# The last attention head and the feed-forward part of a transformer block: another order of steps, a longer lag, and the last two tiles ended one by one

## The chip, the cores and the metric

The kernel runs on one core of one Trainium2 chip. The metric is the time of the program on the device in microseconds, of which the median of three runs stands below. TensorE (PE) multiplies matrices into eight banks of PSUM, VectorE (DVE), ScalarE (ACT) and GpSimd (POOL) do the rest, and SyncE (SP) issues the DMAs. Each engine works off a list of its own in order, and waits on semaphores for the others.

## The reference

One transformer block with its norms behind it, on 1024 tokens of 256 features: 16 attention heads over compressed keys and values, a small sparse attention whose mean is added to the heads, an output projection, a layer norm, a feed-forward part with ternary weights, and a second layer norm. What the change touches is the last of it:

```python
scores = jnp.where(causal[None, None], -jnp.inf, scores)
probs = jax.nn.softmax(scores, axis=-1)
attn = jnp.einsum('bhqk,bhkd->bhqd', probs, v)
...
out = attn.transpose(0, 2, 1, 3).reshape(B, S, NH * VD) @ W_o
...
x = _layernorm(x + attention)
up = jnp.einsum('bsd,ed->bse', x, wu)
gate = jnp.einsum('bsd,ed->bse', x, wg)
hidden = jax.nn.silu(up) * gate
x = _layernorm(x + jnp.einsum('bse,de->bsd', hidden, wd))
```

Here wu, wg and wd are the weights rounded to -1, 0 and 1, times their mean absolute value.

## The kernel before

Everything is float32. Where a product must be exact enough, an operand is held as a high part (rounded to the fast matmul format fp32r) and a low part, and two or three matmuls are added up; so many tiles exist as a pair `Xh`, `Xl`. ScalarE writes the high part out of PSUM by a copy, and VectorE the low part by a subtraction (line 1058 or 1235).

**Order of the work.** The program is a list of steps, written out by hand, that every engine walks through: each step is a tuple (kind, head offset, c), and each engine has, for each kind, its share of instructions and waits. So a step that moves in the list moves on all engines at once. The heads come in pairs; a prologue, the first pair, a loop over six pairs and the last pair `LAST` use `head_steps`, and `EPILOGUE` holds what is left of head 15 and the feed-forward part. A head has eight slots, one for each tile of 128 queries. Slot i is

```python
s += [("qk", h, i), *slots[i][:e], ("exp", h, i), *slots[i][e:]]
```

with e = 2, so two steps stand between a score tile and its exponential.

**Steps of a head.** `qk` i: five matmuls for each 512 keys into SC0 or SC1, and VectorE's masked maximum (line 1121). `exp` i: ScalarE's exponential into Pb (line 959). `tc`: transposes of up to four blocks of Pb on TensorE (line 701), `PTh` by ScalarE, `PTl` by VectorE; tiles 4 to 7 have two such steps each. `pv` g: the product with V for query tiles 2g and 2g+1 (lines 675 to 677), `ATh` and `ATl`. `wo` g: the product with the output weights, and VectorE adds it to `acc` (lines 1270 and 1276). A banked step uses the next of four PSUM banks J0 to J3 and waits until that bank's step four places before has been read.

**Layer norm and feed-forward part.** `ln1` c: statistics of tokens 256c to 256c+255 on VectorE (1218, 1222), then an addition and a power on GpSimd (605, 607). `ln1n` c: VectorE normalises `acc` (1227). `ht` c, for c = 0 and 1, and `h2` c, for 2 and 3: four transposes of the normalised tokens (831, 891), ScalarE's two copies and VectorE's two subtractions (1235), which give `hTh` and `hTl`; these live in the buffers QNh0, QNl0 and QS0, KD0. The steps n = 0 to 31 are 8 blocks of 128 hidden features for each of four groups of 256 tokens:

- `ug` n: eight matmuls, up and gate, into a half of SC0 or SC1 (866, 867). It waits for hidden step n-4; `ug` 0 and 1 also wait for the exponential of tile 6, `ug` 2 and 3 for that of tile 7.
- `m` n, the hidden step: ScalarE's sigmoid (988), then the copy `Hh` of step n-1 (941; names RKh, RKl); VectorE's two products (1191 `QX`, 1194 `CS`); GpSimd's subtraction `Hl` (640; names RQh, RQl). Hh and Hl are rings of eight.
- `dn` n, the down product: four matmuls into J0 and J1 or J2 and J3 (883, 884), added up over eight n. In the list it stands LAG = 5 steps behind `ug`.
- `res`, `ost`, `onorm` q, for two tiles of tokens each: VectorE adds `acc` (1198), takes statistics (1203, 1206), GpSimd makes the inverse deviation, VectorE normalises (1212), and SyncE stores 256 KB (541).

The sigmoid needs another table than the exponential; its load (ACT_TABLE_LOAD) is put directly before the first sigmoid.

## Time and profile before

| | us |
|---|---|
| median of three runs | 727.49 (726.06 to 728.73) |
| the profiled run | 727.64 |
| span of the profiled run | 725.9 |
| TensorE busy | 665.2 (92%) |
| VectorE busy | 469.2 (65%) |
| ScalarE busy | 397.7 (55%) |
| GpSimd busy | 365.8 (50%) |

Times within the execution are counted from the start of the span. A row of the order of time gives start, length, engine, line, operation and tiles, and in square brackets how long the engine stood idle before it and what ended that. Matmuls overlap: a row of 0.28 us is followed by the next 0.12 later. The profile names tiles by their buffers, so the hidden tiles read as RKh, RQh and so on, and the tokens' transposes as QNh, QNl, QS and KD.

### The profile page before, as it was taken

How to read it: one execution, taken by the hardware profiler on the slowest of the kernel's cores; microseconds unless marked ns; L12 is line 12 of the kernel's file. 1: busy time of each engine (PE TensorE's matmuls, PEld its weight loads, DVE VectorE, ACT ScalarE, POOL GpSimd, SP SyncE). 2: the span in 40 equal slices, each digit the busy share in tenths (PEclk: the TensorE clock that was granted, in tenths of full speed). 3: DMA queues.
4: the chain of work that ended last, by engine and by line, in shares of the span. 5: the costliest groups of instructions: out<-in, count | busy, mean ns of one | idle time of the engine just before them, and what ended most of it. 6: DMA issues, size and time to landing. Idle time of an engine off the chain costs nothing.

```text
span 725.9 us, 14196 instructions
## 1 busy us (share of the span) xinstructions
PE 665.2 (92%) x4496; PEld 604.1 (83%) x4496; DVE 469.2 (65%) x1293; ACT 397.7 (55%) x940; POOL 365.8 (50%) x313
## 2 busy tenths in 40 slices
PE   5666799999999999999999999999999999898895
PEld 5646689888988898889888888898889888887895
DVE  2675256666766576666666666666656677895895
ACT  3342254756475647565656565656565658544562
POOL 5522254835474447445744575356536644530563
PEclk9866599999999999999999999999999999999998
DMA  6142310371036103710361037103610373000000
GB/s 203 46 130 75 79 51 1 88 154 52 1 89 153 51 0 87 152 51 0 87 152 51 0 87 152 51 0 87 151 51 0 87 217 87 2 1 1 1 31 30
DMA packets 28719, 50.51 MB, mean 70 GB/s; under 512 B 8976, under 2 KB 19472, under 8 KB 28688
## 3 DMA queue, kind: packets, MB, share of 16 engines
q1 hardware_dynamic: 28688, 50.12, 27.5%
q8 instruction: 17, 0.28, 0.2%
q14 instruction: 14, 0.11, 0.1%
HBM read 15.50 MB, written 1.05 MB: 23 GB/s over the span
## 4 chain that ended last, share of the span: by engine, by line
PE 60%; DVE 13%; ACT 12%; issue 10%; POOL 4%; DMA 1%; DVEq 0%; ACTq 0%; POOLq 0%; SPq 0%
PE J L675 10%; PE J L677 9%; PE J L676 9%; PE J L701 4%; DVE PTl L1058 4%; ACT kvraw L1022 3%; PE SC L692 3%; PE SC L690 3%; PE SC L689 3%; PE SC L691 3%; PE SC L688 3%; POOL rstd L607 3%; ACT Pb L959 3%; ACT PTh L941 2%; PE SC L866 2%
## 5 line engine op out<-in xcount | busy, mean ns | idle before, releaser
L1058 DVE TENSOR_TENSOR PTl<-J,PTh 128x512 fp32r<-128x512 f32 (+1 forms) x192 | 102.5, 554 | 75.1 <-ACT PTh L941 74.4
L959 ACT ACTIVATE Pb<-SC,nm 128x128 f32<-128x128 f32 (+7 forms) x128 | 94.8, 740 | 47.0 <-DVE nm L1121 46.2
L1121 DVE CUSTOM_DVE_ANT_0 SC<-SC,mask 128x128 f32<-128x128 f32 (+7 forms) x128 | 97.4, 761 | 28.7 <-PE SC L692 27.1
L941 ACT ACTIVATE PTh<-J 128x512 fp32r<-128x512 f32 (+1 forms) x192 | 88.3, 492 | 10.3 <-PE J L701 9.5
L701 PE MATMUL J<-ident,Pb 128*128 128x128 f32 x576 | 88.0, 280 | 4.7 <-ACT Pb L959 4.5
L675 PE MATMUL J<-PTh,Vh 128*128 128x256 f32 x320 | 88.0, 275 | 4.0 <-DVE PTl L1058 3.8
L676 PE MATMUL J<-PTl,Vh 128*128 128x256 f32 x320 | 89.6, 280 | 0.0
L677 PE MATMUL J<-PTh,Vl 128*128 128x256 f32 x320 | 89.3, 279 | 0.0
L701 PEld LDWEIGHTS J<-ident,Pb 128*128 128x128 f32 x576 | 64.8, 142 | 11.2 <-ACT Pb L959 5.4
L688 PE MATMUL SC<-KNh,QNh 128*128 128x512 f32 (+1 forms) x192 | 69.1, 360 | 0.0
L675 PEld LDWEIGHTS J<-PTh,Vh 128*128 128x128 f32 x320 | 60.2, 188 | 9.0 <-DVE PTl L1058 6.7
L690 PE MATMUL SC<-KNh,QNl 128*128 128x512 f32 (+1 forms) x192 | 66.8, 348 | 0.0
L689 PE MATMUL SC<-KNl,QNh 128*128 128x512 f32 (+1 forms) x192 | 66.8, 348 | 0.0
L692 PE MATMUL SC<-KL,QS 128*128 128x512 f32 (+1 forms) x192 | 66.8, 348 | 0.0
L691 PE MATMUL SC<-KD,QS 128*128 128x512 f32 (+1 forms) x192 | 66.7, 347 | 0.0
L941 ACT ACTIVATE ATh<-J 128x256 fp32r<-128x256 f32 x64 | 24.5, 383 | 73.1 <-PE J L677 72.4
L676 PEld LDWEIGHTS J<-PTl,Vh 128*128 128x128 f32 x320 | 60.3, 188 | 0.6
L677 PEld LDWEIGHTS J<-PTh,Vl 128*128 128x128 f32 x320 | 60.6, 190 | 0.0
L1058 DVE TENSOR_TENSOR ATl<-J,ATh 128x256 fp32r<-128x256 f32 x64 | 27.0, 422 | 49.5 <-ACT ATh L941 49.5
L1276 DVE SCALAR_TENSOR_TENSOR acc<-J,rs,acc 128x256 f32<-128x256 f32 x128 | 56.1, 480 | 2.6
L941 ACT ACTIVATE kvraw<-J 128x512 f32<-128x512 f32 x32 | 19.2, 599 | 65.6 <-PE J L677 65.6
L1022 ACT ACTIVATE kvraw<-kvraw,nmr,rstd 128x128 f32<-128x128 f32 x128 | 52.6, 487 | 2.5 <-POOL nmr L654 2.5
(267 smaller groups left out, 1916.7 us busy)
## 6 DMA issues: line engine op xcount, KB each, us to landing
KD<-RKh SPq DMA_DIRECT2D x32, 256.0 KB, 4.5
KL<-RKl SPq DMA_DIRECT2D x32, 256.0 KB, 5.1
KX<-KX SPq DMA_DIRECT2D x16, 256.0 KB, 2.4
QX<-QX SPq DMA_DIRECT2D x16, 256.0 KB, 2.4
QS<-RQh SPq DMA_DIRECT2D x16, 256.0 KB, 4.0
QS<-RQl SPq DMA_DIRECT2D x16, 256.0 KB, 4.5
r_kv<-in_L_attn_W_ckv SPq DMA_DIRECT2D x8, 384.0 KB, 3.4
r_qn<-in_L_attn_W_qT SPq DMA_DIRECT2D x16, 128.0 KB, 2.7
```

The source lines that it names most:

```text
L675: mm(o, lhsT=wh, rhs=xh, start=start, stop=False)
L676: mm(o, lhsT=wh, rhs=xl, start=False, stop=False)
L677: return mm(o, lhsT=wl, rhs=xh, start=False, stop=stop)
L688: mm(o[:, k], lhsT=QNh[b][:, q], rhs=KNh[b][:, k], start=True, stop=False)
L689: mm(o[:, k], lhsT=QNh[b][:, q], rhs=KNl[b][:, k], start=False, stop=False)
L690: mm(o[:, k], lhsT=QNl[b][:, q], rhs=KNh[b][:, k], start=False, stop=False)
L692: last = mm(o[:, k], lhsT=QS[b][:, q], rhs=KL[b][:, k], start=False, stop=True)
L701: last = pe.transpose(o[:, tile(j - 4 * c)], Pb[i % 2][:, tile(j)], ident[:, :])
L941: return act.activation(o, i, ACT.Copy)
L959: act.activation(Pb[i % 2][:, w], SC[i % 2][:, w], ACT.Exp, bias=nm[:, i % 2:i % 2 + 1], scale=-1.0, accum_out=sm[:, b, i:i + 1]).then_inc ...
L1058: dve.tensor_tensor(o, i, h.bitcast(F32), ALU.subtract).then_inc(done[kind], 1)
L1121: dve.tensor_tensor_reduce(out=SC[i % 2][:, w], in0=SC[i % 2][:, w], in1=mask[:, 128 * (7 - i):S], scale=-SCALE, scalar=HIGH, op0=ALU.add, ...
```

## The change

1. In the last head, `ln1 0` moves from slot 5 to 4, `ln1n 0` from 6 to 5, `ht 0` from 7 to 6, and `ug 0` and `ug 1` from the epilogue into slot 7, ahead of `ln1n 1`.
2. The epilogue begins with `wo 2`, the transposes of tile 7, `ug 2`, `ht 1`, `m 0` and `ug 3`, and `pv 3` comes behind `m 0`; the sigmoid's table load moves with `m 0`.
3. LAG is 7 instead of 5. `dn 0` comes behind `ug 7`, and eight down products stand behind `ug 31` where six stood.
4. `m 31` comes ahead of `res 2`, `ost 2` and `onorm 2`, and the last two tiles of tokens have steps of their own: `last 0` and `last 1` (sum, statistics; on GpSimd the inverse deviation of one tile) and `lnorm 0` and `lnorm 1` (normalise one tile, store 128 KB). TensorE signals tile 6 with a semaphore of its own, `dn_first`, in the middle of `dn 31`.

The core of the diff:

```diff
-LAG = 5
+LAG = 7
...
-                    add(5, True, ("ln1", 0, 0))
-                    add(6, True, ("ln1n", 0, 0), ("ln1", 0, 1))
-                    add(7, True, ("ht", 0, 0), ("ln1n", 0, 1))
+
+            def late_steps():
+
+                add(4, True, ("ln1", 0, 0))
+                add(5, True, ("ln1n", 0, 0))
+                add(6, True, ("ht", 0, 0), ("ln1", 0, 1))
+                add(7, True, ("ug", 0, 0), ("ug", 0, 1), ("ln1n", 0, 1))
...
             if last:
                 mlp_steps()
+                if b == 1:
+                    late_steps()
...
-            if q >= 1:
+            if q in (1, 2):
                 a += {1: [one("res", q - 1)], 2: [one("ost", q - 1)], 4: [one("onorm", q - 1)]}.get(e, [])
...
-        EPILOGUE = [one("ug", 0), one("ug", 1), *t(NH - 1, 7), ("wo", NH - 1, 2), one("ht", 1), ("pv", NH - 1, 3), one("m", 0),
-                    one("ln1", 2), one("ug", 2), one("ug", 3), one("m", 1), ("wo", NH - 1, 3), one("ln1n", 2), one("ug", 4),
-                    one("m", 2), one("ln1", 3), one("ug", 5), one("m", 3), one("dn", 0), one("ug", 6), one("ln1n", 3),
-                    one("m", 4), one("dn", 1)]
+        EPILOGUE = [("wo", NH - 1, 2), *t(NH - 1, 7), one("ug", 2), one("ht", 1), one("m", 0), one("ug", 3), ("pv", NH - 1, 3),
+                    one("m", 1), one("ln1", 2), one("ug", 4), one("m", 2), ("wo", NH - 1, 3), one("ln1n", 2), one("ug", 5),
+                    one("m", 3), one("ln1", 3), one("ug", 6), one("m", 4), one("ln1n", 3)]
         for n in range(7, NM):
             EPILOGUE += mlp_steps_of(n)
-        EPILOGUE += [one("m", NM - 2), one("onorm", 2), one("m", NM - 1)] + [one("dn", n) for n in range(NM - LAG, NM)]
-        EPILOGUE += [one("res", 3), one("ost", 3), one("onorm", 3)]
+        EPILOGUE += [one("m", NM - 2), one("dn", NM - 7), one("m", NM - 1), one("res", 2), one("ost", 2), one("onorm", 2)]
+        EPILOGUE += [one("dn", n) for n in range(NM - 6, NM)] + [one("last", 0), one("last", 1), one("lnorm", 0), one("lnorm", 1)]
...
+                    if kind == "last":
+                        q = slice(6 + c, 7 + c)
+                        inv_std(mv2[:, q, 1], ve2[:, q], rsd2[:, q], y_ag, c + 4, y_ve, y_rsd, c + 4)
...
+                    if n == NM - 1 and t == 0:
+                        last.then_inc(dn_first, 1)
...
+                    if kind == "last":
+                        t = 6 + c
+                        dve.wait_ge((dn_first, dn_ready)[c], (1, NM)[c])
+                        dve.scalar_tensor_tensor(yo[:, t, :], J[2 + c][:, 0:D], scl[:, 2:3], acc[:, t, :],
+                                                 ALU.mult, ALU.add).then_inc(y_done, 1)
+                        dve.wait_ge(y_done, t + 1)
+                        dve.bn_stats(st2[:, t, :], yo[:, t, :]).then_inc(y_st, 1)
+                        dve.wait_ge(y_st, t + 1)
+                        dve.bn_aggr(mv2[:, t, :], st2[:, t, :]).then_inc(y_ag, 1)
```

TensorE, from the transposes of tile 6 to the last product with V, first before and then after. `ident,acc` are the transposes `ht` (the first of them in the row before; after the change it stands some thirty rows further up, not shown), `SC0<-` and `SC1<-` the up products, `ident,Pb0` and `ident,Pb1` the transposes of tiles 6 and 7, `ABh1,ATh0` the output product 2, and `PTh,Vh1` the products with V. Line numbers of after are 12 to 14 higher.

```order
L701 MATMUL J3<-ident,Pb0 128x128 x4
L701 MATMUL J0<-ident,Pb0 128x128 x3
L831 MATMUL J1<-ident,acc 128x128 x4
L866 MATMUL SC0<-QNh0,xTh 128x256
...
L867 MATMUL SC0<-KD0,xTl 128x256
L701 MATMUL J2<-ident,Pb1 128x128 x4
L701 MATMUL J3<-ident,Pb1 128x128 x4
L675 MATMUL J0<-ABh1,ATh0 128x256
...
L831 MATMUL J1<-ident,acc 128x128 x4
L675 MATMUL J2<-PTh,Vh1 128x256
```

```order
L713 MATMUL J0<-ident,Pb0 128x128 x4
L713 MATMUL J1<-ident,Pb0 128x128 x3
L878 MATMUL SC0<-QNh0,xTh 128x256
...
L879 MATMUL SC0<-KD0,xTl 128x256
L687 MATMUL J2<-ABh1,ATh0 128x256
...
L713 MATMUL J3<-ident,Pb1 128x128 x4
L713 MATMUL J0<-ident,Pb1 128x128 x4
L878 MATMUL SC1<-QNh0,xTh 128x256
...
L843 MATMUL J1<-ident,acc 128x128 x4
L878 MATMUL SC1<-QNh0,xTh 128x256
...
L687 MATMUL J2<-PTh,Vh1 128x256
```

Before, `ht 0` stands between the transposes of tile 6 and up product 0; after, up products 0 and 1 follow these transposes directly, output product 2 stands ahead of the transposes of tile 7, and up products 2 and 3 stand ahead of the last product with V.

ScalarE, from the copy of tile 7's transposes to the first sigmoids, before and after. `QNh0` and `QNl0` are the copies of `ht 1`, `ATh1` that of the last product with V, `QX<-SC0,scl` the sigmoids.

```order
L941 ACTIVATE PTh<-J2 128x4x128
L941 ACTIVATE PTh<-J3 128x4x128
L941 ACTIVATE QNh0<-J1 128x256
L941 ACTIVATE QNl0<-J1 128x256
L941 ACTIVATE ATh1<-J2 128x256
L988 ACT_TABLE_LOAD
L988 ACTIVATE QX<-SC0,scl 128x256 x2
```

```order
L955 ACTIVATE PTh<-J1 128x3x128
L955 ACTIVATE PTh<-J3 128x4x128
L955 ACTIVATE PTh<-J0 128x4x128
L955 ACTIVATE QNh0<-J1 128x256
L955 ACTIVATE QNl0<-J1 128x256
L1002 ACT_TABLE_LOAD
L1002 ACTIVATE QX<-SC0,scl 128x256
L955 ACTIVATE ATh1<-J2 128x256
L1002 ACTIVATE QX<-SC0,scl 128x256
```

The table load and sigmoid 0 stood behind `ATh1` and now stand ahead of it.

VectorE, the end of its list, before and after. `QX` and `CS` are a hidden step, `KX<-J` the sum with `acc`, `KX<-KX` the normalisation.

```order
L1206 BN_AGGR mv<-st 128x2 x2
L1191 SCALAR_TENSOR_TENSOR QX<-SC,scl,QX 128x256
L1194 SCALAR_TENSOR_TENSOR CS<-SC,scl,QX 128x256
L1212 TENSOR_SCALAR KX<-KX,mv,rsd 128x256 x2
L1191 SCALAR_TENSOR_TENSOR QX<-SC,scl,QX 128x256
L1194 SCALAR_TENSOR_TENSOR CS<-SC,scl,QX 128x256
L1198 SCALAR_TENSOR_TENSOR KX<-J,scl,acc 128x256 x2
L1203 BN_STATS st<-KX 128x6 x2
L1206 BN_AGGR mv<-st 128x2 x2
L1212 TENSOR_SCALAR KX<-KX,mv,rsd 128x256 x2
```

```order
L1208 SCALAR_TENSOR_TENSOR CS<-SC,scl,QX 128x256
L1212 SCALAR_TENSOR_TENSOR KX<-J,scl,acc 128x256 x2
L1217 BN_STATS st<-KX 128x6 x2
L1220 BN_AGGR mv<-st 128x2 x2
L1240 TENSOR_SCALAR KX<-KX,mv,rsd 128x256 x2
L1225 SCALAR_TENSOR_TENSOR KX<-J,scl,acc 128x256
L1228 BN_STATS st<-KX 128x6
L1230 BN_AGGR mv<-st 128x2
L1225 SCALAR_TENSOR_TENSOR KX<-J,scl,acc 128x256
L1228 BN_STATS st<-KX 128x6
L1230 BN_AGGR mv<-st 128x2
L1234 TENSOR_SCALAR KX<-KX,mv,rsd 128x256 x2
```

Before, hidden step 31 stands behind the normalisation of tiles 4 and 5; after, sum, statistics and normalisation of tiles 4 and 5 stand behind it, and tiles 6 and 7 follow one by one.

## Rows read from the trace of the kernel before

**Rows 1.** The page, parts 1 and 2: span and granted clock in 40 slices.

```profile
span 725.9 us, 14196 instructions
...
PEclk9866599999999999999999999999999999999998
```

**Rows 2.** Windows: us, busy (x instructions) of TensorE, its weight loads, VectorE, ScalarE, GpSimd; clock; DMA.

```profile
48.00:52.00 4.00, 3.84 (x11) 3.09 (x12) 3.87 (x7) 0.61 (x2) 0.00 (x0) 0.64 0.00 0
...
655.90:658.70 2.80, 0.09 (x1) 0.00 (x0) 2.02 (x6) 1.99 (x5) 0.00 (x0) 1.00 0.00 0
...
660.00:663.40 3.40, 3.40 (x19) 3.40 (x17) 0.41 (x1) 0.79 (x2) 0.00 (x0) 0.51 0.00 0
```

**Rows 3.** Order of time, TensorE, 650 to 668: start, length, engine, line, operation [idle <-releaser].

```profile
650.24 0.40 PE L688 MATMUL SC<-KNh,QNh 128*128 128x512 f32 x1
...
654.61 0.95 PE L701 MATMUL J<-ident,Pb 128*128 128x128 f32 x7
...
655.39 0.60 PE L831 MATMUL J<-ident,acc 128*128 128x128 f32 x4
...
658.73 0.39 PE L866 MATMUL SC<-QNh,xTh 128*128 128x256 f32 x1 [2.74 <-DVE KD L1235]
...
664.68 0.36 PE L675 MATMUL J<-PTh,Vh 128*128 128x256 f32 x1 [0.15 <-DVE PTl L1058]
...
667.53 0.33 PE L866 MATMUL SC<-QNh,xTh 128*128 128x256 f32 x1
```

**Rows 4.** Order of time, TensorE, in the prologue, the last pair and the feed-forward part.

```profile
48.16 0.47 PE L675 MATMUL J<-qch,Wqph 128*128 128x512 f32 x1 [1.98 <-DVE qcs L1058]
...
631.63 0.36 PE L675 MATMUL J<-PTh,Vh 128*128 128x256 f32 x1 [1.12 <-DVE PTl L1058]
...
679.77 0.39 PE L866 MATMUL SC<-QNh,xTh 128*128 128x256 f32 x1 [0.33 <-DVE CS L1194]
...
684.62 0.28 PE L866 MATMUL SC<-QNh,xTh 128*128 128x256 f32 x1
...
713.03 0.27 PE L866 MATMUL SC<-QNh,xTh 128*128 128x256 f32 x1
...
713.97 0.28 PE L883 MATMUL J<-KNh,RKh 128*128 128x256 f32 x1
...
718.83 0.38 PE L883 MATMUL J<-KNl,RKl 128*128 128x256 f32 x1 [1.90 <-POOL RQl L640]
```

**Rows 5.** Order of time, VectorE, 648 to 683.

```profile
648.61 0.29 DVE L1058 TENSOR_TENSOR PTl<-J,PTh 128x128 fp32r<-128x128 f32 x1 [0.35 <-ACT PTh L941]
...
668.15 0.42 DVE L1058 TENSOR_TENSOR ATl<-J,ATh 128x256 fp32r<-128x256 f32 x1 [1.89 <-ACT ATh L941]
...
670.86 0.74 DVE L1218 BATCH_NORM_STATS2 st<-acc 128x6 f32<-128x256 f32 x2
...
672.95 0.88 DVE L1276 SCALAR_TENSOR_TENSOR acc<-J,rs,acc 128x256 f32<-128x256 f32 x2
...
677.65 1.16 DVE L1227 TENSOR_SCALAR acc<-acc,mvl,rsd 128x256 f32<-128x256 f32 x2 [0.40 <-POOL rsd L607]
...
681.42 0.47 DVE L1191 SCALAR_TENSOR_TENSOR QX<-SC,scl,QX 128x256 f32<-128x256 f32 x1
...
682.33 0.47 DVE L1191 SCALAR_TENSOR_TENSOR QX<-SC,scl,QX 128x256 f32<-128x256 f32 x1
```

**Rows 6.** Order of time, ScalarE, last exponential and table load.

```profile
655.76 1.11 ACT L959 ACTIVATE Pb<-SC,nm 128x1024 f32<-128x1024 f32 x1
...
668.13 1.28 ACT L988 ACT_TABLE_LOAD   x1
```

**Rows 7.** Order of time, ScalarE and VectorE, from the last sigmoid to the end.

```profile
714.17 0.48 ACT L988 ACTIVATE QX<-SC,scl 128x256 f32<-128x256 f32 x1 [0.60 <-PE SC L867]
...
719.60 0.88 DVE L1198 SCALAR_TENSOR_TENSOR KX<-J,scl,acc 128x256 f32<-128x256 f32 x2 [2.08 <-PE J L884]
...
722.54 0.74 DVE L1212 TENSOR_SCALAR KX<-KX,mv,rsd 128x256 f32<-128x256 f32 x2 [1.19 <-POOL rsd L607]
```

More of the change, by code:

```diff
@@ L240, in attention_and_mlp @@
                                                                   sem("hid_done"), sem("hh_done"), sem("hl_done"))
+        dn_first = sem("dn_first")
         dn_ready, y_done, y_st, y_ag, y_ve, y_rsd, y_ln, stored = (sem("dn_ready"), sem("y_done"), sem("y_st"),
@@ L538, in run @@
                         sp.dma_start(raw[c].rearrange("p (k n) -> p k n", n=src.shape[2]), src).then_inc(ld_mlp[c], 16)
+                    if kind == "lnorm":
+                        sp.wait_ge(y_ln, c + 4)
+                        sp.dma_start(out[768 + 128 * c:896 + 128 * c, :], yo[:, 6 + c, :]).then_inc(stored, 16)
                     if kind == "onorm":
@@ L548, in _ @@
             run(EPILOGUE, 0)
-            sp.wait_ge(stored, 64)
+            sp.wait_ge(stored, 80)
         LD_C, LD_SIDE, LD_W0 = 16 * 8, 16 * 8, 16 * 7
@@ L1207, in run @@
                         ins.then_inc(y_ag, 1)
+                    if kind == "last":
[7 more added lines that the diff above has]
+                        dve.bn_aggr(mv2[:, t, :], st2[:, t, :]).then_inc(y_ag, 1)
+                    if kind == "lnorm":
+                        t = 6 + c
+                        dve.wait_ge(y_rsd, c + 4)
+                        dve.tensor_scalar(yo[:, t, :], yo[:, t, :], mv2[:, t, 0:1], rsd2[:, t:t + 1], ALU.subtract,
+                                          ALU.mult).then_inc(y_ln, 1)
                     if kind == "onorm":
```

## The prediction

> **What bounds the kernel now.** I read the page first: the span is 725.9 us, and the clock row reads 9 of 10 in every slice behind the prologue but the last [rows 1]; a drop of some 3 us inside a slice of 18 does not show there, so finer windows are needed. The change touches nothing before the last head, at about 640 us, so I then read the engines' order of time from there to the end. The reader is to see four stretches in it.
>
> First, TensorE runs dense through the last score tile, the third product with V and the transposes, and then stands still for 2.74 us before up product 0, released by VectorE's `KD`, the low half of the transposed tokens [rows 3]. `KD` is late because the step `ht 0` stands behind the last exponential, which starts at 655.76 [rows 6]. Second, that stall drops the clock: 0.51 of full speed from 660.0 to 663.4, at 3.40 of 3.40 us busy, after 0.09 of 2.80 us busy [rows 2]. That is the level of 1.2 GHz instead of 2.4, and it loses half of 3.4 us, 1.7 us. Third, from 668 to 680 the feed-forward part starts up: up product n waits for hidden step n-4, VectorE makes one hidden step per 0.91 us [rows 5], with the layer norms, the last output product and the splits between them, and TensorE waits for it. The last such wait is of 0.33 us, at 679.77 [rows 4]. Fourth, from there to 713.03 TensorE is dense: 20 steps (one up, one down product each) from 684.62 to 713.03 are 1.42 us each [rows 4]. At the end down product 31 waits 1.90 us for the chain of hidden step 31 [rows 4], and the output norm of two tiles and a store follow.
>
> **The transposed tokens and two up products come forward.** Nothing is added here; the steps change places on all engines. From the start of the last score tile at 650.24 [rows 3] I lay the new order with the old durations: `ht 0` 0.48 (its row at 655.39 is busy 0.60 with 0.12 of overlap), score tile, product with V and seven transposes 5.15 (655.39 less 650.24), up products 0 and 1 at 0.94 each (713.97 less 713.03, [rows 4]), output product 2 at 0.79 (six matmuls at 0.119, the rate of the 24 from 664.68 to 667.53, and 0.08 to begin), eight transposes 0.9 (seven took 0.78 from 654.61), up product 2, `ht 1` 0.48, up product 3, and the last product with V 2.85. It ends at 664.65, where before it ended at 667.53.
>
> Is each input there? `ht 0` on TensorE waits for the first layer norm, which VectorE and GpSimd now make one slot earlier; VectorE's idle pieces in that slot, such as 0.35 us at 648.61 [rows 5], take the 0.95 us that come in, and the norm ends about 649.9, 0.3 before it is asked for. Its copies stand on ScalarE between the exponential of tile 6 and that of tile 7, its splits on VectorE ahead of the last score's reduction: 0.67 us more there, but the norm of tiles 0 and 1 has left that place (0.69), so the last exponential slips by the 0.4 us that TensorE's own order adds, from 655.76 to about 656.2, done at 657.4. The eight transposes ask for it at 658.5. `KD` is there at about 653.6, up product 0 asks at 655.9: the 2.74 us stall goes, and with it the clock drop behind it. The cover is therefore 1.1 us at the exponential and 2.3 us at `KD`; where one is gone, the excess is paid one to one.
>
> **The sigmoid's table.** Its load takes 1.28 us and stood straight behind the copy of the last product with V [rows 6], so VectorE waited for the first sigmoid. Now it stands behind `ht 1`, whose copies end about 661.6; sigmoid 0 can start at 662.9 and hidden step 0 ends at 664.4, while TensorE is busy to 664.65 with the last product with V. The load costs nothing there, with 0.25 us to spare. The Trainium skill, "ScalarE: Activation LUTs", section "What ACT_TABLE_LOAD costs", counts about 2.66 us for a switch, with a drain. The row here has 1.28; by the page's price the sum would be about 1.1 us worse.
>
> **The start-up is then VectorE's.** Before, the split `ATl` of the last product with V began at 668.15 [rows 5], 0.62 behind the last matmuls of that product, and hidden step 7 ended at 683.32 (682.33 and 0.51 and 0.48). Now `ATl` begins at 665.27 and VectorE is free at 665.65. What it has to do up to hidden step 7: seven hidden steps (1 to 7) at 0.91, two layer-norm statistics at 0.94 (two of 0.74 busy and aggregates), one output add with its reciprocal 1.05, one normalisation 0.69 without and one 1.08 with GpSimd beside it, and with 0.40 of waiting for GpSimd's `rsd` (677.65), one split pair 0.67 [rows 5]: 12.1 us. Hidden step 7 ends at 677.8, 5.5 us earlier. Lag 7 takes down products 0 and 1 out of this stretch, which TensorE spends waiting anyway. Up product 9 starts behind hidden step 5, at 675.35; with down 2, the `h2` transposes, up 10 and down 3 (0.94, 0.48, 0.48, 0.94, 0.48) up product 11 starts at 678.65. It started at 684.62: **5.97 us earlier**, 0.95 of it work that the lag has put off to the end.
>
> In this stretch TensorE idles for about 0.75 and then 1.55 us around up products 6 and 7. An idle of 2.74 us dropped the clock; so did one of 1.98 (0.64 over 48 to 52 [rows 2, 4]); one of 1.12 did not [rows 4]. Ours lie between, close together, so I take a drop as somewhat likelier than not. It would fall where TensorE has slack, and laying up 7, down 0 and `h2` at half speed I find 0.4 us of loss, up to 1.0 if it comes two products later. I take **0.4** and keep 0 to 1.7.
>
> **The middle.** The 20 steps stay at 1.42 us: VectorE needs 8 x 0.91 and about 2.6 for the output norm per eight steps, 9.9 against TensorE's 11.4. The ring of eight hidden tiles allows lag 7: when ScalarE writes tile n, down product n-8 has been issued before up product n. Up product 31 starts at 713.03 - 5.97 + 0.4 = 707.46.
>
> **The end.** With eight down products behind up product 31 (3.8 us), the chain of hidden step 31 is there before TensorE asks for it, so its 1.90 us wait goes. But what is late next? VectorE: `last 0` stands behind `onorm 2`, which waits for GpSimd behind `res 2` and `ost 2`. From sigmoid 31, 1.14 behind the start of up product 31 (714.17 [rows 7]), now at 708.6: sigmoid and hidden step 1.42; `res 2` with its statistics 1.76 and GpSimd 1.18 (719.60 to 722.54, of which the last 1.18 are the wait for `rsd` [rows 7]); `onorm 2` 0.66; `last 0` and `last 1`, one after the other in three dependent operations each (0.48, 0.41, 0.17 and gaps of 0.04), 1.1 each; GpSimd 1.18; `lnorm 1` 0.43; store 2.62 (725.9 less 723.28). That is 11.45 us where 11.73 stood (725.9 less 714.17): **0.3 us** gained. TensorE is done 2.5 us before `last 1` starts, so ending the tiles one by one earns nothing by itself; the end gains since up product 31 no longer has 0.95 us of down products before it, which is in the 5.97. The halved last store is not in the trace; I take it at the full one's price, since that is the nearest row, with -0.5 to +0.3 as bounds. The extra store and GpSimd's two more pairs lie under `last 1`.
>
> **Sum.** 5.97 - 0.4 + 0.3 = 5.9 us. The profiled run took 727.64, 1.7 more than its span and 0.15 above the median of 727.49; from the median the forecast is **721.6 us**.
>
> **The rivals.**
> - The forecast, 720.3 to 722.8: chance 0.60. For it speaks that each stall has a releaser whose new place is known.
> - Better, 719.4 to 720.3: the clock holds and the smaller store lands sooner. Chance 0.12.
> - The first sigmoid is late: `ht 1` slips past the 0.25 us of cover, and hidden step 0 falls into VectorE's full stretch, at 0.91 and up to the 1.3 us of a load before it: 723.8 at most. Chance 0.05.
> - The switch holds ScalarE longer than the load's own row, say for twice its 1.28 us: 1.1 us past the cover, 722.7. Against it: between the copy before the load and the load there is no gap. Chance 0.05. (By the table page of the Trainium skill named above, this is what a switch costs.)
> - The clock costs more, or VectorE's stretch does: a second drop before up product 11, or one reaching into the dense part, 1.7 us each, or VectorE slowed by GpSimd: 723.3 to 725. Chance 0.08.
> - The change doesn't do what it says: the order of waits in ScalarE's queue (the `ht 0` copies stand ahead of the copy of the product with V and of the last exponential) gives back what the earlier start earns. It costs 4 us only if the norm's end slips from 649.9 to 654; then 725.5 to 729. Chance 0.06.
> - Slower: the clock drops around 671 and stays down. At 48 to 52 it was low with 3.84 of 4 us busy [rows 2], so being busy again does not at once lift it. Each us at half costs 0.5 once TensorE is the bound; it eats the 5.9 and 2.2 more when it lasts 16 us, giving 730 and above. Against it: the drop of 660.0 ended after 3.4 us of the same kind of matmuls. Chance 0.04.
>
> **The numbers.** About 0.3% (2.2 us) is what a measurement of this kernel tells from no change. Faster by more than that: the first five, 0.90; within it 0.06; slower 0.04. The range 719.5 to 724.6 leaves out the last two, the top of the fifth and a tip of the second.
>
> **What would show it.** After: no idle above 0.5 us between the last score tile and the last product with V, and full clock there; table load near 661.6; hidden step 7 ending near 677.8 and up product 11 starting near 679; no wait of TensorE behind up product 31; VectorE, not TensorE, ahead of `last 0`, and about 11.4 us from sigmoid 31 to the end. Wrong would be: a stall before `ht 0` near 650, a low clock in the dense part, or a hidden step 0 behind the last product with V.

## The result, and the profile after

The changed kernel takes **719.58 us**, the median of nine runs (717.91 to 724.32), where the kernel before, run nine times beside it, takes 727.49 (724.88 to 728.73). The ratio is 0.991, with a 95% interval of 0.989 to 0.993: 6.4 us less, 4.9 to 7.8. The profiled execution took 718.92 us. From its page, the lines that answer to [rows 1]:

```profile
span 717.1 us, 14199 instructions
...
PEclk9866599999999999999999999999999999999998
```

The spans differ by 8.8 us (725.9 less 717.1), more than the ratio says. To see why, I split both executions at a mark: VectorE's reduction of the score tile of queries 768 to 895 in the last head. Of what the change moves, only the statistics and the normalisation of the first layer norm (`ln1 0`, `ln1n 0`) stand ahead of it, and the times below show that they cost nothing there. A row ahead of it is the first score tile of all. The order of time, before and then after:

```profile
84.77 0.31 PE L688 MATMUL SC<-KNh,QNh 128*128 128x128 f32 x1
...
649.77 1.10 DVE L1121 CUSTOM_DVE_ANT_0 SC<-SC,mask 128x896 f32<-128x896 f32 x1
```

```profile
82.22 0.31 PE L700 MATMUL SC<-KNh,QNh 128*128 128x128 f32 x1
...
647.20 1.09 DVE L1135 CUSTOM_DVE_ANT_0 SC<-SC,mask 128x896 f32<-128x896 f32 x1
```

So 2.57 us of the 8.8 were there at the mark, and 2.55 already at the first score tile, where the two kernels issue the same things; the last section says what they are. **Behind the mark it is 76.13 us before (725.9 less 649.77) and 69.90 after**, 6.2 less. All that follows is counted from this mark, so that what an execution wins or loses in the prologue stays out.

TensorE, the rows that answer to [rows 3, 4]: up product 0, the two waits of the start-up (ahead of up products 6 and 7), up products 11 and 31, and the down products' last part:

```profile
653.27 0.36 PE L878 MATMUL SC<-QNh,xTh 128*128 128x256 f32 x1
...
665.83 0.38 PE L878 MATMUL SC<-QNh,xTh 128*128 128x256 f32 x1 [0.62 <-DVE CS L1208]
...
668.48 0.54 PE L878 MATMUL SC<-QNh,xTh 128*128 128x256 f32 x1 [1.44 <-DVE CS L1208]
...
676.70 0.28 PE L878 MATMUL SC<-QNh,xTh 128*128 128x256 f32 x1
...
705.12 0.27 PE L878 MATMUL SC<-QNh,xTh 128*128 128x256 f32 x1
...
709.78 0.28 PE L896 MATMUL J<-KNl,RQl 128*128 128x256 f32 x1
```

The 2.74 us before up product 0 are gone, and so are the 1.90 us before down product 31; the two waits that are left between the last score tile and the end are of 0.62 and 1.44 us. The windows, to set beside [rows 2]:

```profile
655.90:658.90 3.00, 3.00 (x28) 3.00 (x28) 2.78 (x7) 1.54 (x4) 0.00 (x0) 1.00 0.00 0
...
668.80:671.80 3.00, 3.00 (x15) 3.00 (x15) 2.54 (x8) 0.85 (x3) 2.44 (x4) 0.50 0.00 0
...
675.00:705.00 30.00, 30.00 (x257) 30.00 (x255) 26.18 (x63) 18.44 (x48) 18.80 (x27) 1.00 0.06 19
```

Where the clock had fallen before, it is full. It falls now behind the wait of 1.44 us: 0.50 over three busy us, 15 matmul rows where the window above has 28. From 675 to 705 TensorE is busy without a gap, at full clock.

ScalarE, the table load, the first sigmoid and the last ([rows 6, 7]), and then VectorE: the low half of the tokens' transposes, the split `ATl`, the last normalisation of a layer norm, hidden step 7, and the end ([rows 5, 7]):

```profile
659.12 1.28 ACT L1002 ACT_TABLE_LOAD   x1
660.41 0.47 ACT L1002 ACTIVATE QX<-SC,scl 128x256 f32<-128x256 f32 x1
...
706.26 0.47 ACT L1002 ACTIVATE QX<-SC,scl 128x256 f32<-128x256 f32 x1 [0.64 <-PE SC L879]
```

```profile
650.52 0.42 DVE L1263 TENSOR_TENSOR KD<-J,QNl 128x256 fp32r<-128x256 f32 x1
...
662.57 0.42 DVE L1072 TENSOR_TENSOR ATl<-J,ATh 128x256 fp32r<-128x256 f32 x1 [0.65 <-ACT ATh L955]
...
670.64 1.16 DVE L1255 TENSOR_SCALAR acc<-acc,mvl,rsd 128x256 f32<-128x256 f32 x2 [0.39 <-POOL rsd L616]
...
674.98 0.48 DVE L1208 SCALAR_TENSOR_TENSOR CS<-SC,scl,QX 128x256 f32<-128x256 f32 x1
...
710.61 0.73 DVE L1240 TENSOR_SCALAR KX<-KX,mv,rsd 128x256 f32<-128x256 f32 x2 [1.18 <-POOL rsd L616]
711.26 0.48 DVE L1225 SCALAR_TENSOR_TENSOR KX<-J,scl,acc 128x256 f32<-128x256 f32 x1
...
712.33 0.45 DVE L1225 SCALAR_TENSOR_TENSOR KX<-J,scl,acc 128x256 f32<-128x256 f32 x1
...
714.57 0.41 DVE L1234 TENSOR_SCALAR KX<-KX,mv,rsd 128x256 f32<-128x256 f32 x1 [0.71 <-POOL rsd L616]
```

The last four rows are the end: VectorE waits 1.18 us for GpSimd inside `onorm 2` and goes on to `last 0` and `last 1`, whose down products TensorE had done at 710.06 (709.78 and 0.28). The last store follows the row of 714.57.

### The profile page after: what moved, and what is told of

Its sections match the earlier page's. It is cut to its first block, busy times and chain, and to the rows that moved or that the text cites. A ratio compares the mean times of both kernels' runs of the same rounds, so it can differ in the third digit from the quotient of the medians.

```text
span 717.1 us, 14199 instructions
## 1 busy us (share of the span) xinstructions
PE 660.8 (92%) x4496; PEld 601.7 (84%) x4496; DVE 468.9 (65%) x1293; ACT 397.2 (55%) x940; POOL 366.0 (51%) x315
## 3 DMA queue, kind: packets, MB, share of 16 engines
HBM read 15.50 MB, written 1.05 MB: 23 GB/s over the span
## 4 chain that ended last, share of the span: by engine, by line
PE 62%; DVE 12%; ACT 11%; issue 9%; POOL 4%; DMA 1%; ACTq 0%; DVEq 0%; POOLq 0%; SPq 0%
PE J L687 10%; PE J L689 10%; PE J L688 10%; PE J L713 4%; DVE PTl L1072 3%; ACT kvraw L1036 3%; PE SC L701 3%; PE SC L704 3%; PE SC L702 3%; PE SC L703 3%; PE SC L700 3%; POOL rstd L616 3%; ACT Pb L973 2%; PE SC L878 2%; PE SC L879 2%
## 5 line engine op out<-in xcount | busy, mean ns | idle before, releaser
L638 POOL CAST Vh<-kvraw 128x1024 fp32r<-128x1024 f32 x16 | 16.6, 1040 | 75.2 <-ACT kvraw L1036 75.2
```

## The experiments

Fourteen executions were profiled, each marked in the same way. All times in the table are in us. The span is printed to a tenth, so the second and the fifth column carry a rounding of 0.05 to either side. "Sigmoid 31" is the start of the last sigmoid; behind it stands the tail, which ends with the span. The idle is TensorE's longest between the last score tile and up product 11, and the last column says whether the granted clock then fell.

| kernel | mark to end | hidden step 7 ends | sigmoid 31 | tail | longest idle | clock fell behind it |
|---|---|---|---|---|---|---|
| before | 76.13 | 33.55 | 64.40 | 11.73 | 2.74 | yes |
| before_again | 76.39 | 33.88 | 64.72 | 11.67 | 2.74 | yes |
| after | 69.90 | 28.26 | 59.06 | 10.84 | 1.44 | yes |
| after_again | 69.51 | 28.05 | 58.58 | 10.93 | 1.43 | no |
| front_only | 71.13 | 28.60 | 59.42 | 11.71 | 1.77 | yes |
| end_only | 74.30 | 32.54 | 63.38 | 10.92 | 2.74 | behind a later idle of 1.43 |
| table_back | 71.83 | 30.38 | 60.91 | 10.92 | 3.30 | yes |
| pair_end | 69.82 | 28.04 | 58.57 | 11.25 | 1.43 | no |
| norm_late | 68.34 | 28.01 | 58.56 | 9.78 | 1.43 | no |
| both | 68.38 | 28.02 | 58.57 | 9.81 | 1.24 | no |
| stall_back | 72.96 | 31.24 | 62.03 | 10.93 | 2.73 | behind a later idle of 1.43 |
| lag5 | 70.32 | 28.65 | 59.48 | 10.84 | 1.76 | yes |
| lag5_norm_late | 69.00 | 28.61 | 59.45 | 9.55 | 1.76 | yes |
| ln_later | 69.01 | 28.62 | 59.43 | 9.58 | 1.76 | yes |

Where two executions have the same steps up to sigmoid 31 and the clock did the same, they agree to 0.03 us (58.56 to 58.58; 59.45 and 59.48). The kernel before scatters by 0.3.

The first question was where the 6.2 us come from. The theory says nearly all from the front: the stall, the table, the lag. The rivals are that the tail carries much of it, that the table did nothing, or that ending the tiles one by one pays.

**front_only**: items 1 and 2 of the change, with the lag of five and the old end.

```diff
-LAG = 7
+LAG = 5
...
-                    one("m", 3), one("ln1", 3), one("ug", 6), one("m", 4), one("ln1n", 3)]
+                    one("m", 3), one("dn", 0), one("ln1", 3), one("ug", 6), one("m", 4), one("dn", 1), one("ln1n", 3)]
...
+        EPILOGUE += [one("m", NM - 2), one("onorm", 2), one("m", NM - 1)] + [one("dn", n) for n in range(NM - LAG, NM)]
+        EPILOGUE += [one("res", 3), one("ost", 3), one("onorm", 3)]
```

> The new order of the last head and of the epilogue's start alone; lag 5 and the old ending (onorm 2 ahead of hidden step 31, tiles 6 and 7 as a pair). Counted from the score reduction of tile 6 in the last head (649.77 before, 647.20 after) to the end of the span, before takes 76.1 us and after 69.9. Theory: nearly all of the gain is made in front; up product 31 starts as early as in after, then the old tail of 11.7 us from sigmoid 31 stands behind it: 70.4 to 70.9. Rival, the gain comes from the lag and the ending: 74 or more.

Measured: 71.13 behind the mark, 5.0 less than before and 0.2 above what I expected; ratio 0.991 (0.989 to 0.993). The order of time of TensorE, down product 0 and down product 31:

```profile
666.86 0.36 PE L895 MATMUL J<-KNh,RKh 128*128 128x256 f32 x1 [1.77 <-DVE acc L1304]
...
711.16 0.39 PE L895 MATMUL J<-KNl,RKl 128*128 128x256 f32 x1 [1.90 <-POOL RQl L649]
```

The front alone brings most of the gain, and the tail is 11.71 as it was. Two things in it were not in my account. Down product 0, which stands ahead of up product 6 as in the kernel before, waits 1.77 us for VectorE, which still has to read the bank of output product 3 (line 1304). And the 1.90 us before down product 31 are back in full.

**end_only**: items 3 and 4, with the old order in the head and at the start of the epilogue. Against the changed kernel:

```diff
-                add(4, True, ("ln1", 0, 0))
-                add(5, True, ("ln1n", 0, 0))
-                add(6, True, ("ht", 0, 0), ("ln1", 0, 1))
-                add(7, True, ("ug", 0, 0), ("ug", 0, 1), ("ln1n", 0, 1))
+                    add(5, True, ("ln1", 0, 0))
+                    add(6, True, ("ln1n", 0, 0), ("ln1", 0, 1))
+                    add(7, True, ("ht", 0, 0), ("ln1n", 0, 1))
```

> The old order in front; lag 7 and the new ending alone. Theory: TensorE's stall of 2.7 us before up product 0 and the clock drop stay, sigmoid 31 comes when it came before, and the tail is 10.8 instead of 11.7 us: 75.2 us from the score reduction of tile 6 to the end. Rival, the ending takes away the stalls of 2.1 us behind up product 31 in full: 73.8 or less.

Measured: 74.30, 1.8 less than before in its trace, and between what I expected and the rival; ratio 0.9995 (0.998 to 1.001), so a run cannot tell it from the kernel before. The tail is 10.92, as in the whole change, 0.8 less than before. The other 1.0 lies ahead of sigmoid 31. The stall's row, the window behind it, and VectorE's row of `ATl`, the split of the last product with V:

```profile
656.40 0.39 PE L874 MATMUL SC<-QNh,xTh 128*128 128x256 f32 x1 [2.74 <-DVE KD L1259]
```

```profile
656.40:659.40 3.00, 3.00 (x25) 3.00 (x26) 0.59 (x2) 0.34 (x1) 0.00 (x0) 1.00 0.00 0
```

```profile
664.58 0.42 DVE L1068 TENSOR_TENSOR ATl<-J,ATh 128x256 fp32r<-128x256 f32 x1 [1.88 <-ACT ATh L951]
```

The same 2.74 us stall stands before up product 0, and this time the clock behind it is 1.00. The stall does not always cost the clock. `ATl` stands ahead of every down product, so the lag cannot touch it, and it begins 17.18 behind the mark (664.58 less 647.40) where it began 18.38 behind it before (668.15 less 649.77) and 18.68 in before_again: the clock's share is 1.2 to 1.5 there. A later fall, behind an idle of 1.43 us ahead of hidden step 7, is in the 63.38 too.

**table_back**: hidden step 0 (`m 0`), and with it the sigmoid's table load, goes back behind the last product with V.

```diff
-        EPILOGUE = [("wo", NH - 1, 2), *t(NH - 1, 7), one("ug", 2), one("ht", 1), one("m", 0), one("ug", 3), ("pv", NH - 1, 3),
-                    one("m", 1), one("ln1", 2), one("ug", 4), one("m", 2), ("wo", NH - 1, 3), one("ln1n", 2), one("ug", 5),
+        EPILOGUE = [("wo", NH - 1, 2), *t(NH - 1, 7), one("ug", 2), one("ht", 1), one("ug", 3), ("pv", NH - 1, 3),
+                    one("m", 0), one("m", 1), one("ln1", 2), one("ug", 4), one("m", 2), ("wo", NH - 1, 3), one("ln1n", 2), one("ug", 5),
```

> After, with hidden step 0 (and with it the table load) behind the last product with V again. Theory, VectorE is the bound from that product on: the load of 1.28 us and the hidden step of 0.91 come back into its stretch, 2.0 to 2.4 us more than after, 72.0 to 72.3 from the score reduction of tile 6 to the end. Rival, the lookahead of four up products hides the load: under 70.4.

Measured: 71.83; ratio 0.992 (0.990 to 0.994). The load starts 15.39 behind the mark instead of 11.92, and up product 4 now waits 3.30 us for hidden step 0 (TensorE's row and ScalarE's):

```profile
666.82 0.39 PE L878 MATMUL SC<-QNh,xTh 128*128 128x256 f32 x1 [3.30 <-DVE CS L1208]
...
663.96 1.28 ACT L1002 ACT_TABLE_LOAD   x1
```

Sigmoid 31 comes 1.85 us later than in the changed kernel, with the clock fallen in both. So of the 5.3 us that the front gains in like executions (64.40 less 59.06), 1.85 belong to the load of 1.28 and the hidden step that moves with it; the run does not part the two. It is a little less than I expected.

**pair_end**: the last two tiles end as one pair again.

```diff
-        EPILOGUE += [one("dn", n) for n in range(NM - 6, NM)] + [one("last", 0), one("last", 1), one("lnorm", 0), one("lnorm", 1)]
+        EPILOGUE += [one("dn", n) for n in range(NM - 6, NM)] + [one("res", 3), one("ost", 3), one("onorm", 3)]
```

> After, with tiles 6 and 7 ended as a pair (sum, statistics, normalisation of both, one store of 256 KB) instead of one by one. Theory: VectorE is late anyway behind onorm 2, so ending them one by one earns only what the smaller GpSimd pair and the smaller last store save: 0.3 to 0.6 us more than after, 70.2 to 70.5. Rival, it earns the chain of one tile, about 1.1: 71.0.

Measured: 69.82 with the clock full (58.57 at sigmoid 31), so it is set against after_again, at 69.51 with a full clock too (further down). What I expected was counted from the 69.90 with the clock fallen. The tail is 11.25 where the one-by-one ending has 10.84 and 10.93; ratio 0.990 (0.987 to 0.992). VectorE's last rows:

```profile
711.31 0.73 DVE L1240 TENSOR_SCALAR KX<-KX,mv,rsd 128x256 f32<-128x256 f32 x2 [1.18 <-POOL rsd L616]
711.96 0.87 DVE L1212 SCALAR_TENSOR_TENSOR KX<-J,scl,acc 128x256 f32<-128x256 f32 x2
...
714.89 0.73 DVE L1240 TENSOR_SCALAR KX<-KX,mv,rsd 128x256 f32<-128x256 f32 x2 [1.18 <-POOL rsd L616]
```

From the end of `onorm 2` to the start of the last normalisation it is 2.85 us here (714.89 less 712.04), 3.23 in the changed kernel (714.57 less 711.34); but the pair's last normalisation is 0.32 longer, and its store of 256 KB lands later: 718.2 less 715.62 is 2.58, where the changed kernel has 717.1 less 714.98, 2.12. Ending one by one loses 0.4 on VectorE and wins 0.8 behind it, 0.3 to 0.4 in all.

**before_again and after_again**: both kernels once more, nothing changed, to see what one execution differs from the next.

> The kernel before, unchanged, for a second trace. In the six traces so far the first score tile starts at 82.0 to 84.8 us, latest in the one trace of before, in a part that the change does not touch. Theory, this is scatter: here it starts somewhere in 82 to 85 again, and 76.1 us (75 to 76.5) pass from the score reduction of tile 6 to the end. Rival, the kernel before is late there every time: 84.5 or more again.

> The changed kernel, unchanged, for a second trace. Theory: from the score reduction of tile 6 to the end 69.4 us if the idle of 1.44 us before up product 7 does not drop the clock in this execution, 69.9 if it does.

Measured: 76.39 and 69.51 behind the mark; ratios to the kernel before 1.001 (0.999 to 1.003) and 0.992 (0.989 to 0.994). The change itself repeats. What does not is the clock: behind the same idle it fell in the first execution of the changed kernel and not in the second (the order of time, and the window behind it).

```profile
671.30 0.38 PE L878 MATMUL SC<-QNh,xTh 128*128 128x256 f32 x1 [1.43 <-DVE CS L1208]
```

```profile
671.50:674.50 3.00, 3.00 (x27) 3.00 (x27) 2.54 (x8) 1.95 (x6) 2.46 (x4) 1.00 0.00 0
```

Sigmoid 31 starts at 58.58 instead of 59.06, so the fall costs **0.48 us** here. The gain behind the mark is 6.2 to 6.5 us with the fall and 6.6 to 6.9 without.

**norm_late**: `onorm 2` behind `last 1`. The theory was that VectorE's 1.18 us of waiting inside `onorm 2` bounds the tail and can be filled by the last sums; the rival, that TensorE's down products bound it next.

```diff
-        EPILOGUE += [one("m", NM - 2), one("dn", NM - 7), one("m", NM - 1), one("res", 2), one("ost", 2), one("onorm", 2)]
-        EPILOGUE += [one("dn", n) for n in range(NM - 6, NM)] + [one("last", 0), one("last", 1), one("lnorm", 0), one("lnorm", 1)]
+        EPILOGUE += [one("m", NM - 2), one("dn", NM - 7), one("m", NM - 1), one("res", 2), one("ost", 2)]
+        EPILOGUE += [one("dn", n) for n in range(NM - 6, NM)] + [one("last", 0), one("last", 1), one("onorm", 2), one("lnorm", 0), one("lnorm", 1)]
```

> After, with the normalisation of tiles 4 and 5 (onorm 2) behind last 1 on VectorE, so that last 0 no longer stands behind its wait for GpSimd. Theory, that wait of 1.18 us and the 0.65 of the normalisation held back last 0: 1.2 to 1.5 us less from sigmoid 31 to the end, 9.4 to 9.6 instead of 10.84. Rival, GpSimd or the store is the bound there: 10.5 or more.

Measured: 68.34, the tail 9.78, 1.1 less than in after_again, where 1.2 to 1.5 were expected; ratio 0.993 (0.991 to 0.996). VectorE's rows of `last 0`, `onorm 2` and the last normalisations:

```profile
708.42 0.48 DVE L1225 SCALAR_TENSOR_TENSOR KX<-J,scl,acc 128x256 f32<-128x256 f32 x1 [0.43 <-PE J L896]
...
710.55 0.72 DVE L1240 TENSOR_SCALAR KX<-KX,mv,rsd 128x256 f32<-128x256 f32 x2
711.18 0.94 DVE L1234 TENSOR_SCALAR KX<-KX,mv,rsd 128x256 f32<-128x256 f32 x2
```

The wait for GpSimd is gone, and `last 0` now waits 0.43 for TensorE. So it was VectorE's wait that bound the end of the changed kernel, and both have a share once it is filled. VectorE ends 712.12 less 646.26, 65.86 behind the mark, and 67.31 in after_again: 1.45 less. What is missing of it at the end is the store's. From the end of the last normalisation to the end of the span it is 2.5 us here and 2.2 in after_again. The three last stores stand closer together here, and the two of 128 KB take 2.1 us from issue to landing, 1.7 in the changed kernel:

```profile
out<-KX SPq DMA_DIRECT2D x2, 128.0 KB, 2.1
```

That the nearness of the stores is what makes them longer is argued from these two kernels, not tested alone. The timed ratio doesn't show the 1.1 us; the scatter of the prologue (last section) is larger than that.

**both**: norm_late, and down products 0 and 1 in the idle before up product 7. This asks of the lag: the prediction has 0.95 us of these two products among its 5.97.

```diff
-            if n >= LAG:
+            if n >= LAG + 2:
...
-                    one("m", 3), one("ln1", 3), one("ug", 6), one("m", 4), one("ln1n", 3)]
+                    one("m", 3), one("ln1", 3), one("ug", 6), one("m", 4), one("dn", 0), one("dn", 1), one("ln1n", 3)]
```

> norm_late, and down products 0 and 1 behind up product 6, in TensorE's idle 1.44 us before up product 7, instead of behind up products 7 and 8. Theory: the 0.95 us of these two products leave the dense stretch and the clock stays up until up product 7; sigmoid 31 comes 0.5 to 1.4 us earlier than in after (59.1 us behind the score reduction of tile 6), with the tail of norm_late: 67.2 to 68.0 in all. Rival, VectorE is the bound up to up product 10 and the idle only moves behind up product 8 (and may drop the clock there): sigmoid 31 within 0.3 us of after's.

Measured: sigmoid 31 at 58.57, the same as without, so the rival came; ratio 0.989 (0.986 to 0.992). TensorE's waits show where the work went:

```profile
669.63 0.38 PE L878 MATMUL SC<-QNh,xTh 128*128 128x256 f32 x1 [0.32 <-DVE CS L1208]
...
673.92 0.39 PE L878 MATMUL SC<-QNh,xTh 128*128 128x256 f32 x1 [1.24 <-DVE CS L1208]
```

The first row is up product 7, whose idle of 1.43 us is cut to 0.32; the second is up product 9, which had none and now waits 1.24. The lag is still seven, and as many down products stand ahead of up product 31 as before; two of them only moved out of the work behind up products 7 and 8. That moved nothing: up to here VectorE sets the time.

**stall_back**: `ht 0` goes back to slot 7, directly ahead of `ug 0`; the rest of the change stays.

```diff
-                add(6, True, ("ht", 0, 0), ("ln1", 0, 1))
-                add(7, True, ("ug", 0, 0), ("ug", 0, 1), ("ln1n", 0, 1))
+                add(6, True, ("ln1", 0, 1))
+                add(7, True, ("ht", 0, 0), ("ug", 0, 0), ("ug", 0, 1), ("ln1n", 0, 1))
```

> After, with ht 0 back behind the transposes of tile 6 (its split again behind the last exponential), up products 0 and 1 behind it. Theory, this place is what made the stall of 2.7 us: it comes back before up product 0, and everything up to sigmoid 31 is 2.5 to 2.9 us later than in after (58.6 us behind the score reduction of tile 6 with a full clock), and up to 1.7 more where the clock drops behind it: 61.1 to 63.2. Rival, the moved up products 2 and 3 take the stall up: sigmoid 31 before 60.0.

Measured: 72.96, sigmoid 31 at 62.03; ratio 0.995 (0.993 to 0.998). The stall is there again, and the clock falls later, behind an idle of 1.43 us:

```profile
658.67 0.39 PE L878 MATMUL SC<-QNh,xTh 128*128 128x256 f32 x1 [2.73 <-DVE KD L1263]
```

```profile
673.60:676.60 3.00, 2.71 (x13) 2.71 (x14) 2.54 (x9) 1.20 (x3) 1.99 (x4) 0.56 0.00 0
```

Against the changed kernel with the same fall of the clock it is 2.97 us later at sigmoid 31. The stall's own 2.7 us come back nearly one to one, and of the front's 5.3 us they are the largest part. With the 1.85 of table_back and the 0.42 of lag5 (next) they make 5.2: the three parts, each undone alone, account for the front to within the 0.3 by which the kernel before scatters.

**lag5**: the whole change but for the lag.

```diff
-LAG = 7
+LAG = 5
...
-                    one("m", 3), one("ln1", 3), one("ug", 6), one("m", 4), one("ln1n", 3)]
+                    one("m", 3), one("dn", 0), one("ln1", 3), one("ug", 6), one("m", 4), one("dn", 1), one("ln1n", 3)]
...
+        EPILOGUE += [one("m", NM - 2), one("m", NM - 1), one("res", 2), one("ost", 2), one("onorm", 2)]
+        EPILOGUE += [one("dn", n) for n in range(NM - 5, NM)] + [one("last", 0), one("last", 1), one("lnorm", 0), one("lnorm", 1)]
```

> After with lag 5 (five down products behind up product 31 and its own 26, down 0 and 1 in the start-up), the rest of the new ending kept. Theory: VectorE is the bound in the start-up and at the end, and what takes the wait of 1.9 us off the path is that hidden step 31 stands ahead of onorm 2, not the lag: the same as after, 69.4 to 70.0 from the score reduction of tile 6. Rival, the lag hides the chain of hidden step 31: 70.4 or more.

Measured: 70.32, sigmoid 31 at 59.48, a tail of 10.84; ratio 0.988 (0.983 to 0.992). Its 70.32 lies past the end of what I expected, and just short of the rival. TensorE, down products 0 and 31, then the window in which the clock is low and the one from down product 0 to up product 9:

```profile
669.50 0.36 PE L895 MATMUL J<-KNh,RKh 128*128 128x256 f32 x1 [1.76 <-DVE acc L1304]
...
711.99 0.39 PE L895 MATMUL J<-KNl,RKl 128*128 128x256 f32 x1 [0.45 <-POOL RQl L649]
```

```profile
670.70:673.70 3.00, 3.00 (x16) 3.00 (x16) 2.54 (x9) 1.20 (x3) 1.98 (x4) 0.54 0.00 0
669.50:676.30 6.80, 6.80 (x45) 6.80 (x45) 5.74 (x16) 2.45 (x8) 2.48 (x5) 0.75 0.00 0
```

The tail is that of lag seven, within the rounding. Of the 1.90 us before down product 31, which front_only has at the same lag, 0.45 are left; the two kernels differ there in that `m 31` comes ahead of `res 2` and `onorm 2`. So 1.45 of the end's wait went with the place of `m 31`; the lag takes the last 0.45, and these cost nothing while VectorE is bound. Lag seven with the old place of `m 31` was not run. What the lag does is at the front: without it down product 0 stands ahead of up product 6 and waits 1.76 us for VectorE's reading of `acc`'s bank. It costs 0.4 us with the clock fallen in both (59.48 against 59.06), and 0.9 against the execution in which it stayed up.

The second window shows on what the 0.4 hangs. From down product 0 to up product 9 TensorE is busy for all of 6.80 us, at a mean clock of 0.75, so 1.7 us of them are the fall's. By these numbers, an estimate, up product 9 would be asked for 24.9 us behind the mark at full clock, and in after_again it waits for VectorE until 25.6. So lag five would cost nothing with the clock up. The four executions with its idle of 1.76 or 1.77 us all had the fall.

**lag5_norm_late**: both edits, to see whether their effects add.

> Lag 5 together with onorm 2 behind last 1. In norm_late last 0 waited 0.43 us for TensorE, which had eight down products behind up product 31. Theory: with lag 5 down product 31 ends 0.3 to 0.5 earlier, so the tail from sigmoid 31 is 9.3 to 9.6 us where norm_late had 9.8: lag 7 then costs. Rival, TensorE waits for the chain of step 31 longer than it saves: 9.8 or more.

Measured: 69.00, the tail 9.55; ratio 0.990 (0.985 to 0.995). Sigmoid 31 is at 59.45, as in lag5, and the tail is 0.2 shorter than in norm_late. They add, and at the end lag five is now the better one, as I expected: `last 0` waits 0.20 us for TensorE where norm_late has 0.43, with two down products fewer behind up product 31. So lag seven earns 0.4 in the front and gives 0.2 back here.

**ln_later**: lag5_norm_late, and the last layer norm's normalisation (`ln1n 3`) one step later, behind `m 5`, so that VectorE reaches hidden step 5 sooner.

```diff
-            a = [one("ug", n), one("m", n - 2)]
+            a = [one("ug", n), one("m", n - 2)] + ([one("ln1n", 3)] if n == 7 else [])
...
-                    one("m", 3), one("ln1", 3), one("ug", 6), one("m", 4), one("ln1n", 3)]
+                    one("m", 3), one("dn", 0), one("ln1", 3), one("ug", 6), one("m", 4), one("dn", 1)]
```

> lag5_norm_late, with the normalisation ln1n 3 one hidden step later on VectorE, behind hidden step 5. In after it waits 0.39 us for GpSimd's rsd and then takes 1.16 instead of 0.75. Theory, VectorE's start-up stretch is the bound: sigmoid 31 comes 0.6 to 1.1 us earlier, 57.5 to 58.0 us behind the score reduction of tile 6, and the whole is 66.9 to 67.5. Rival, another wait takes its place (h2, or hidden step 3's chain on GpSimd): 58.3 or more.

Measured: sigmoid 31 at 59.43, nothing gained; ratio 0.987 (0.983 to 0.991). VectorE's rows:

```profile
673.98 0.91 DVE L1255 TENSOR_SCALAR acc<-acc,mvl,rsd 128x256 f32<-128x256 f32 x2
...
676.12 0.42 DVE L1263 TENSOR_TENSOR QS<-J,QNh 128x256 fp32r<-128x256 f32 x1 [1.23 <-ACT QNl L955]
```

The normalisation takes 0.91 us here, without GpSimd's wait of 0.39 ahead of it, but the split behind it waits 1.23 us for ScalarE's copies, and those for transposes that TensorE reaches late. What is saved at one place is waited for at the next. TensorE is late because it is in the same dense 6.80 us as in lag5, at a clock of 0.75 (669.90 to 676.70); whether the edit gains at full clock no run shows.

## Why the prediction was right, and where it was not

The number held, but not by much: 721.6 was forecast and 719.58 measured, 0.08 above the lower end of the range (719.5) and in the band of the rival "better". Of that rival's two conditions, the smaller store landed sooner in both profiled executions of the changed kernel, and the clock held in one of them. From the ratio the gain is 6.4 us, where 5.9 was forecast; the medians' 7.9 carry the scatter of the prologue (last section). Behind the mark the forecast was 70.2 (76.13 less 5.9), and the trace has 69.90. There two errors of opposite sign partly cancel, which is luck: sigmoid 31 comes 0.2 later than forecast, and the tail is 0.6 shorter. Step by step, from the mark (the forecast's times less 649.77, the trace's less 647.20):

| step | forecast | after |
|---|---|---|
| `KD` ready | 3.8 | 3.74 |
| up product 0 starts | 6.1 | 6.07 |
| table load starts | 11.8 | 11.92 |
| `ATl` starts | 15.50 | 15.37 |
| hidden step 7 ends | 28.0 | 28.26 |
| up product 11 starts | 29.3 (28.88 and 0.4 for the clock) | 29.50 |
| up product 31 starts | 57.69 | 57.92 |
| sigmoid 31 starts | 58.8 | 59.06 |
| tail | 11.45 | 10.84 |

**The stall and its clock**: right. The 2.74 us are gone and nothing stands in their place; stall_back brings 2.97 back. But the drop of the clock that I counted with the stall is not certain: the same 2.7 us were followed by one in both executions of the kernel before and by none in end_only and stall_back.

**The table**: right. The load starts 0.1 us from where it was laid, its cover holds, and table_back pays 1.85 for its old place. Of the price of a switch: the load's row is 1.28 us, and the sigmoid's row begins 1.29 behind the start of the load, 1.30 in the kernel before. The Trainium skill, "ScalarE: Activation LUTs", section "What ACT_TABLE_LOAD costs", adds some 1.4 us of drain to each switch; no row here has it, and the rival that rested on it did not come. (That rival's price was 0.1 too high by its own numbers: 1.28 less the cover of 0.25 is 1.0.)

**VectorE's stretch**: right in kind and size. 12.1 us were summed up from 0.38 behind the start of `ATl` to the end of hidden step 7; the trace has 12.5 (675.46 less 662.95) with the clock fallen. Where it stayed up, hidden step 7 ends 28.01 to 28.05 behind the mark, the forecast to the hundredths. TensorE's idles were forecast at 0.75 and 1.55 and are 0.62 and 1.44.

**The clock**: sized at 0.4, measured at 0.48. In three of the six executions with the idle of 1.43 or 1.44 it did not fall at all.

**The lag**: this step was wrong, though the sum did not show it. The prediction says of the 5.97 us at up product 11 "0.95 of it work that the lag has put off to the end", and of the tail that "the end gains since up product 31 no longer has 0.95 us of down products before it". But the stretch up to there was VectorE's, by the prediction's own words, and work that TensorE does not do in it earns nothing. In the run "both", two down products leave the work behind up products 7 and 8 for the idle ahead of it, and sigmoid 31 moves by 0.01 at most. The 5.97 came right because it was laid from hidden step 5, not because of the 0.95. What the lag does, and I did not see, is to keep down product 0 from standing ahead of up product 6, where it waits for VectorE's reading of output product 3; lag5 shows 0.4 us for that, with the clock fallen in both, and by the estimate there nothing at full clock. The same step said that the 1.90 us wait goes since eight down products stand behind up product 31; lag5 has five, and the wait is 0.45 and costs nothing. 1.45 of it went since `m 31` no longer stands behind `res 2` and `onorm 2`.

**The tail**: the term of 0.3 measured some 0.8 (11.73 and 11.67 before, 10.84 and 10.93 after). Mis-sized was the store above all, taken at 2.62 us and measured at 2.12, at the edge of the bounds. The other 0.1 is spread over the steps; the largest piece is the last wait for GpSimd, 0.07 shorter than laid. "Ending the tiles one by one earns nothing by itself" is wrong by pair_end: it earns 0.3 to 0.4, by a shorter last normalisation and the smaller store, though not by the earlier start that one might look for, since VectorE reaches `last 0` only 1.2 us after TensorE has done everything.

**What is left of the difference in us**: 8.8 in the two profiled spans, of which 2.6 are the prologue's. The medians differ by 7.9 and the ratio says 6.4; a median of three, as the forecast was made from, carries the same scatter.

Two kernels are better than the changed one in the trace alone: norm_late and both end 68.3 to 68.4 us behind the mark, 1.1 less than after_again. Their timed ratios (0.993 and 0.989, each some 0.0025 to either side) do not tell them from the changed kernel's.

## What to carry to other kernels

Before pricing work that is taken out of a stretch, ask which engine sets that stretch: two down products were worth nothing on TensorE while VectorE was bound. Putting them off paid, 0.4 us, only because the first of them had stood, waiting, ahead of something that others needed, and because the clock then fell. When a stall goes, check each edit that goes with it by undoing it alone; a sum can come right with a wrong term in it. And compare executions from a mark behind whatever varies by itself, since here the start of the program moves by 3.3 us, more than most of the edits are worth.
